# Denominator sums in pairs of heads on GpSimd, and VectorE multiplying the output bank out of PSUM

## What is computed

```python
def _tc_rmsnorm(x, t, gw, gb, bw, bb):
    g = (t @ gw.T + gb)[:, None, :]
    b = (t @ bw.T + bb)[:, None, :]
    inv_rms = jax.lax.rsqrt(jnp.mean(x * x, axis=-1, keepdims=True) + EPS)
    return g * x * inv_rms + b

def _attention(x, Wq, Wk, Wv, Wo):          # 16 heads of 32
    q, k, v = ...                           # x @ W.T, split into heads
    attn = jnp.einsum('blhd,bmhd->bhlm', q, k) / scale
    p = jax.nn.softmax(attn, axis=-1)
    o = jnp.einsum('bhlm,bmhd->blhd', p, v).reshape(B, L, D)
    return o @ Wo.T

x1 = x0 + _attention(_tc_rmsnorm(x0, t, ...), Wq, Wk, Wv, Wo)
y = x1 + silu(h @ gate_w.T) * (h @ hid_w.T) @ out_w.T    # h = _tc_rmsnorm(x1, ...)
out = x0 + y
```

## Time and profile before

| | us |
|---|---|
| median of 3 runs | 2371.1 |
| lowest, highest | 2369.59, 2376.34 |
| profiled execution | 2371.89 |
| its span | 2370.0 |

### The profile page before, as it was taken

How to read it: one execution, slowest core, us unless ns; L and a number is a source line. 1 busy time by engine, 2 the same in 40 slices (tenths; PEclk the granted TensorE clock), 3 DMA queues, 4 the chain that set the end, 5 groups by cost and what they waited for, 6 DMA issues and landing times.

```text
span 2370.0 us, 38915 instructions
## 1 busy us (share of the span) xinstructions
PE 2247.4 (95%) x10848; PEld 1565.9 (66%) x10848; DVE 1647.2 (70%) x2723; ACT 1283.8 (54%) x2286; POOL 1419.5 (60%) x1331
## 2 busy tenths in 40 slices
PE   5999989999989999899999889999999999999999
PEld 4655447555457554466554468887888788888887
DVE  4777745777736777546777378877887788778877
ACT  3367772567763667735666644363436344544454
POOL 0299981699952899915999846504660367036712
PEclk9999999999999999999999999999999999999999
DMA  6432213322132323132221331146114621363125
GB/s 192 149 96 64 83 34 99 88 77 65 59 103 51 97 56 90 32 112 66 64 54 32 111 138 54 39 153 210 54 36 134 222 65 36 111 201 109 43 88 179
DMA packets 96454, 221.94 MB, mean 94 GB/s; under 512 B 15712, under 2 KB 15712, under 8 KB 94560
## 3 DMA queue, kind: packets, MB, share of 16 engines
q1 hardware_dynamic: 95792, 212.93, 30.3%
q10 hardware_dynamic: 432, 6.29, 0.7%
HBM read 144.71 MB, written 24.12 MB: 71 GB/s over the span
## 4 chain that ended last, share of the span: by engine, by line
PE 75%; DVE 8%; issue 7%; ACT 4%; POOL 2%; SPq 2%; DMA 2%; DVEq 0%; ACTq 0%; POOLq 0%
PE bank L1869 26%; PE bank L1883 12%; PE bank L976 9%; PE bank L1100 8%; PE bank L1055 7%; PE bank L1161 6%; DVE pmax L800 3%; PE bank L1086 3%; PE bank L1065 2%; POOL sums L539 2%; SPq L381 2%; ACT qk_hi L617 1%; PE bank L1041 1%; DVE ow L1689 1%; DMA wo_raw<-in_out_w 1%
## 5 line engine op out<-in xcount | busy, mean ns | idle before, releaser
L800 DVE TENSOR_REDUCE pmax<-bank 128x1 f32<-128x512 f32 x1024 | 645.4, 683 | 177.5 <-PE bank L1055 171.5
L539 POOL TENSOR_TENSOR sums<-sums,probs_up 128x512 f32<-128x512 f32 x432 | 540.3, 1285 | 0.1
L1055 PE MATMUL bank<-ks,qs 96*128 96x512 f32 x1024 | 421.2, 422 | 36.2 <-DVE pmax L800 34.6
L1161 PE MATMUL bank<-qs,ks 128*128 128x512 f32 x1024 | 421.2, 416 | 15.0 <-ACT probs L701 8.3
L1883 PE MATMUL bank<-ow,aw 128*128 128x512 f32 x1536 | 360.6, 392 | 2.8 <-DVE ow L1689 2.7
L1869 PE MATMUL bank<-H_hi,wt_hi 128*128 128x512 f32 x896 | 350.5, 391 | 8.5 <-DVE H_lo L1724 8.3
L1869 PE MATMUL bank<-H_lo,wt_hi 128*128 128x512 f32 x896 | 349.8, 390 | 0.0
L1869 PE MATMUL bank<-H_hi,wt_lo 128*128 128x512 f32 x896 | 349.6, 390 | 0.0
L701 ACT ACTIVATE probs_up<-bank 128x512 f32<-128x512 f32 x512 | 283.3, 607 | 97.5 <-PE bank L1161 91.2
L701 ACT ACTIVATE probs<-bank 128x512 f32<-128x512 f32 x512 | 286.9, 602 | 86.3 <-PE bank L1161 78.7
L1883 PEld LDWEIGHTS bank<-ow,aw 128*128 128x128 f32 x1536 | 285.0, 188 | 65.3 <-issue 7.1
(11 more groups left out here) (184 smaller groups left out, 3559.3 us busy)
## 6 DMA issues: line engine op xcount, KB each, us to landing
raw<-in_gu_w SPq DMA_DIRECT2D x66, 512.0 KB, 3.8
wo_raw<-in_out_w SPq DMA_DIRECT2D x128, 256.0 KB, 2.8
qs<-qk_hi SPq DMA_DIRECT2D x256, 64.0 KB, 2.0
ks<-qk_hi SPq DMA_DIRECT2D x128, 128.0 KB, 2.4
x<-attn_out SPq DMA_DIRECT2D x10, 1024.0 KB, 9.2
x<-in_x SPq DMA_DIRECT2D x8, 1024.0 KB, 7.5
qs<-qk_lo SPq DMA_DIRECT2D x128, 64.0 KB, 2.0
ks<-qk_lo SPq DMA_DIRECT2D x64, 128.0 KB, 2.4
```

The costliest lines, as they stand in the source:

```text
L539: nc.gpsimd.tensor_tensor(total, first, probs(s, h), ALU.add) \
L800: nc.vector.reduce_max(pmax[:, t, h, hf:hf + 1], mbank[n % MB][:], AX_X).then_inc(sq_done, 1)
L1055: nc.tensor.matmul(mbank[n % MB][:], qs[0:96, u % 3, h, t * P:(t + 1) * P], ks[0:96, u // 2 % 2, h, hf * QB:(hf + 1) * QB], start=True, st ...
L1161: nc.tensor.matmul(sbank[i % SB][:], ks[:, g % 2, h, s * P:(s + 1) * P], qs[:, u % 3, h, :], start=True, stop=True).then_inc(st_ready, 1)
```

## The change

GpSimd's adds take two heads in one instruction (128 x 1024), 12 a unit. The place of the sums of heads 0 and 1 in quad 0 becomes the last quarter of `o` (group 3), except in unit 7, where all sums lie in `sums`, and the first add of each of its quads waits for the read of the one before. GpSimd's multiply goes. ScalarE's copies `output` and `denominators_up` go, and with them the semaphores `od_act`, `den_ready` and `den_up`. VectorE does all four parts of `normalise(u - 1)` in slots 6, 7, 8 and 9 of unit u, for u from 1 to 7, the second transpose now as a `link`; the last part multiplies `obank` by `den` and writes `o`. The values of pair 0 (slot 13) wait for that multiply. The last unit's normalisation stays where it was, in the new form.

```diff
+NORMALISE_AT = {(1, 2): 0, (1, 3): 1, (2, 0): 2, (2, 1): 3}
...
+HEADS = 2
+SUMS = QUADS * (QT - 1) * GH // HEADS
...
-    def sum_place(quad, h):
-        return yout[:, 0, :] if (quad, h) == (0, 0) else sums[:, h, :]
+    def probs_of(s, heads):
+        return probs_parts[s % 4 // 2][:, s % 2, HEADS * heads:HEADS * heads + HEADS, :]
+
+    def sum_places(u, quad, heads):
+        if u < NU - 1 and quad == 0 and heads == 0:
+            return o[:, NG - 1, :].rearrange("p (h c) -> p h c", h=HEADS)
+        return sums[:, HEADS * heads:HEADS * heads + HEADS, :]
...
-        def normalise(b, u):
-
-            pool.wait_ge(od_act, b * NU + (u + 2))
-            pool.wait_ge(den_ready, b * (NU - 1) + (u + 1))
-            cols = o[:, u // 2, u % 2 * QB:(u % 2 + 1) * QB]
-            nc.gpsimd.tensor_tensor(cols, cols, den[:], ALU.mult).then_inc(on_done, 1)
...
-                    if s == 4 and 0 < u < NU - 1:
-                        normalise(b, u - 1)
...
+                    for heads in range(GH // HEADS if s % QT else 0):
+
+                        pool.wait_ge(st_done, SCORES_T(b, NT + n * GH + HEADS * heads + HEADS) + SB)
...
+                        if s % QT == 1 and (heads == 1 or u == NU - 1):
 
                             pool.wait_ge(w_ready, MISC(b, sums_before(b, u, s // QT)))
...
+                        total = sum_places(u, s // QT, heads)
+                        first = probs_of(s - 1, heads) if s % QT == 1 else total
+                        nc.gpsimd.tensor_tensor(total, first, probs_of(s, heads), ALU.add) \
                             .then_inc(sum_done, 1)
...
-                        if (s, h) == (1, 1) and u:
-                            output(b, u - 1)
-                        if u == NU - 1 and (s, h) == (2, 3):
-                            denominators_up(b)
...
-            elif part == 2 and u == NU - 1:
+            elif part == 2:
                 link(nc.vector.transpose(den[:], pair[:, 1, :].unsqueeze(2).to_broadcast([P, QB // 32, 32])))
...
+                dve.wait_ge(pv_done, b * (NU * PAIRS) + (u + 1) * PAIRS + 2)
                 cols = o[:, u // 2, u % 2 * QB:(u % 2 + 1) * QB]
-                nc.vector.tensor_tensor(cols, cols, den[:] if u == NU - 1 else mspare[:], ALU.mult).then_inc(on_done, 1)
+                nc.vector.tensor_tensor(cols, obank[:], den[:], ALU.mult).then_inc(on_done, 1)
...
-                        if s == 3 and 0 < u < NU - 1 and h < 3:
-                            normalise(b, u - 1, h)
-                        if s == 2 and u == NU - 1 and h < 3:
-                            normalise(b, u - 1, h)
-                        if (u, s, h) == (NU - 1, 3, 0):
-                            normalise(b, u - 1, 3)
+                        if u and (s, h) in NORMALISE_AT:
+                            normalise(b, u - 1, NORMALISE_AT[s, h])
...
-                pe.wait_ge(od_act, b * NU + (u + 1))
+                pe.wait_ge(on_done, b * NU + (u + 1))
```

More of the change, by code:

```diff
@@ L165 @@
 SCORES_Q = Counter(0, NU * NMAX + NT)
-SUMS = QUADS * (QT - 1) * GH
+HEADS = 2
+SUMS = QUADS * (QT - 1) * GH // HEADS
 assert QT * QUADS == NS
-LINKS_PER_BATCH = NU * (2 + 2) + 1
+LINKS_PER_BATCH = NU * (2 + 3)
 HEAD_INC = 3 * 16
@@ L201, in sums_done @@
 def sums_done(b, u, s, h):
-    return b * (NU * SUMS) + (SUMS * (u + 1) + GH * (s // QT * (QT - 1) + max(s % QT, 1) - 1) + h + 1)
+    return b * (NU * SUMS) + (SUMS * (u + 1) + GH // HEADS * (s // QT * (QT - 1) + max(s % QT, 1) - 1) + h // HEADS + 1)
 def act_before(b, tile):
@@ L517, in batch @@
                         inverse_root(b, b * 2 + 3)
-                    if s == 4 and 0 < u < NU - 1:
-                        normalise(b, u - 1)
                     if n == NU * NS - 1:
                         pool.wait_ge(sum_done, sums_done(b, u, s - 1, GH - 1))
-                        pool.sem_inc(sum_done, GH)
+                        pool.sem_inc(sum_done, GH // HEADS)
                         break
[L525 to L531, removed]
+                    for heads in range(GH // HEADS if s % QT else 0):
+                        pool.wait_ge(st_done, SCORES_T(b, NT + n * GH + HEADS * heads + HEADS) + SB)
+                        if (u, s, heads) == (0, 1, 0):
+                            for w in range(2):
+                                pool.wait_ge(w_lo[w], 2)
+                        if s % QT == 1 and (heads == 1 or u == NU - 1):
                             pool.wait_ge(w_ready, MISC(b, sums_before(b, u, s // QT)))
                         if s % QT > 1:
[L536 to L539, removed]
+                            pool.wait_ge(sum_done, sums_done(b, u, s - 1, HEADS * heads))
+                        total = sum_places(u, s // QT, heads)
+                        first = probs_of(s - 1, heads) if s % QT == 1 else total
+                        nc.gpsimd.tensor_tensor(total, first, probs_of(s, heads), ALU.add) \
                             .then_inc(sum_done, 1)
@@ L548, in scalar_part @@
         act.sem_inc(st_done, ST_LEAD + SB)
-        act.sem_inc(od_act, 1)
         def square(b, hf, t):
@@ L696, in batch @@
                         act.wait_ge(st_ready, SCORES_T(b, i + 1))
-                        if s % QT != 1:
+                        if s % QT != 1 and h % HEADS == 0:
                             act.wait_ge(sum_done, sums_done(b, u, s - QT, h) if s >= QT
@@ L728, in batch @@
                             act.dma_start(wv[:].bitcast(F32), wv_dram).then_inc(wv_loaded, 16)
-            output(b, NU - 1)
             output_hi(b, len(SPLIT_AT))
@@ L1064, in denominators @@
             for h in range(GH):
-                last = nc.tensor.matmul(wbank[DH * h:DH * h + DH, :], ones[:], sum_place(quad, h), start=True,
+                last = nc.tensor.matmul(wbank[DH * h:DH * h + DH, :], ones[:], sum_places(u, quad, h // HEADS)[:, h % HEADS, :], start=True,
                                         stop=not direct)
@@ L1202, in attention_program @@
         "stacks": [(s, NB * NU * HEAD_INC) for s in q_stacked] + [(s, NB * NG * HEAD_INC) for s in k_stacked],
-        "values": [(pv_done, NB * NU * PAIRS + 2), (od_act, NB * NU + 1), (sum_done, sums_done(b, NU - 1, NS - 1, GH - 1))],
+        "values": [(pv_done, NB * NU * PAIRS + 2), (on_done, NB * NU + 1), (sum_done, sums_done(b, NU - 1, NS - 1, GH - 1))],
         "denominators": [(w_dve, MISC_DVE(b, dve_before(b, ("D", NU - 1, 1)) + 1))],
```

18 lines of the change are left out of this document (removed).

## The result

The changed kernel took 2414.6 us (median of four executions, 2407.7 to 2417.2), the kernel before beside it 2370.4: the ratio is 1.0171, 95% interval 1.0155 to 1.0187. The forecast was 2383.6 with a range from 2360 to 2397. The sign was right; the loss, forecast at 12.5 us, is 41 to 44.

What follows compares the result with a forecast made beforehand. TensorE, 95% busy, was taken as the bound, locally held by VectorE's reductions. Units 1 and 3 +19.2, unit 2 +6.8, unit 4 -5.6, unit 5 -0.35, unit 6 -7.1, unit 7 -0.4: +12.5 on 2371.1, 2383.6 us; range 2360 to 2397.

Steps and rivals of the forecast that it cites:

- The bound and the place: Units 1 and 3: VectorE's reduction of slot 10 gates slot 13's maxima product, then pair 0's values; +2.4 us each.
- rival 1: Slots 6 to 9, units 1 to 3: VectorE's added work absorbed, 0.6 us of 2.4 left; about 2358, chance 0.25.
- rival 2: GpSimd paces every unit through sums and denominators; 3 us per unit would go, 2330 us or below, chance 0.04.
- rival 3: A paired GpSimd add costs 2.8 us; waits for sums stay and about 5 us come on top, 2395, chance 0.08.
- the lower bound for the add: GpSimd's paired add costs at least 2.13 us: twice 1.285 less a whole 0.43 of fixed cost; 2.35 was taken.
- The burst: VectorE's four normalisation parts in slots 6 to 9: 2.4 us; +2.4 in units 1 and 3, +1.7 in unit 2.
- The second halves: Slots 14 to 21, freed of transposes and reciprocal: unit 4 -1.3 us in three batches, -1.7 in the last.
- The waits for sums: TensorE's 9.2 us of waits for GpSimd's sums all go: 7.0 in the last batch, the rest in unit 6.
- Units 5 and 6: Both halves over four batches, including sums' waits removed: unit 5 -0.35 us, unit 6 -7.1 us.

Runs made afterwards that it cites:

- the kernel with added products: Changed kernel plus 88 unread 512-column products in slots 10 to 13 of units 1 and 3 and 10 to 12 of unit 2: 2401.8 us.
- the shorter burst: Changed kernel without the first transpose and the reciprocal in units 1 to 7; second transpose and multiply stay in slots 8 and 9: 2381.6 us.

## Why the prediction was right or wrong

**The bound and the place: right.** "The chain through VectorE already sets this stretch": red(10) sets max(13), max(13) the values. Burst and waits lie where they were put, and rival 1 (absorbed), rival 2 (GpSimd paces every unit) and rival 3 (adds of 2.8 us) are all out: 2.6 us per burst arrive at TensorE in units 1 and 3, the pairs alone left these units at 0.0, and an add is 2.38. The 0.43 us of fixed cost in the lower bound for the add stands in no row; rows 3 give 1.285 - 512 x 0.00216 = 0.18. It did not enter the sum.

**The burst: right, a little small.** Units 1 and 3 at 2.4 became 2.6 (2.4 in the last batch): 20.6 for 19.2. Unit 2 at 1.7 became 2.0: 8.1 for 6.8. These are the numbers at the high clock.

**The second halves: right in size in unit 4, in part by luck.** Forecast was 0 for slots 6 to 13 and, for slots 14 to 21, -1.3 and in the last batch -1.7. Measured, from values to values, are +0.35 (+0.10 in the last batch) and -1.46, -1.88, -1.50 and -1.64; the whole first stretches sum to -5.3 for -5.6. But 1.1 of the 5.3 comes from an earlier transfer of keys, which the prediction did not have.

**The clock: the step that failed.** The prediction priced each wait by VectorE's queue alone and never asked what waits do to TensorE's granted clock. In the profiled execution that is 13.0 us (14.8 - 10.3 in unit 1, 18.8 - 10.3 in unit 3, by the kernel with added products), the largest term there is. The mean of 0.992 before could have raised the question. Most of what it lacks to 1.00 lies outside the attention units (0.93 over the 116 us ahead of them), but in unit 6's second stretch the clock is at 0.92 in the first batch and 0.91 in the third, 1.00 in the second, and the stretch lasts 17.83, 18.09 and 16.46 us. The Trainium skill, page "TensorE: Matmul & The Clock Gate", section "A second HAM failure mode: psum-queue depth-cycling", says that an engine that idles briefly and often between groups of products can swing between its two clock levels. The traces agree: here, four waits of 0.25 to 0.70 us in four slots.

Unit 2 has three of these waits, 0.59, 0.25 and 0.69, and no fourth, since a projection stands in slots 12 and 13; its clock stays at 1.00 in all four batches (2.06, 2.09, 2.13, 1.84):

```profile
512.00:516.00 4.00, 3.06 (x11) 1.84 (x12) 3.81 (x7) 1.49 (x4) 4.00 (x3) 1.00 0.77 169
516.00:520.00 4.00, 4.00 (x26) 1.92 (x25) 1.87 (x3) 0.91 (x2) 4.00 (x2) 1.00 0.07 14
```

That is no rule by the number of waits. Unit 5 of the last batch has three smaller ones (0.50, 0.16 and 0.60) and its stretch is at 0.90, and with the shorter burst two waits were enough in two of eight cases.

**The waits for sums: mis-sized.** Forecast: all 9.2 us go. Measured: 4.3 stay, 3.5 in units 5 and 6 and 0.8 in unit 7. The prediction had six adds of 2.35 run back to back once slot 21 is done. GpSimd in the last batch shows two of them standing apart:

```profile
1336.92 2.37 POOL L535 TENSOR_TENSOR sums<-probs 128x1024 f32<-128x1024 f32 x1
1340.99 2.36 POOL L535 TENSOR_TENSOR sums<-probs 128x1024 f32<-128x1024 f32 x1 [1.70 <-ACT probs L681]
1343.32 9.35 POOL L535 TENSOR_TENSOR sums<-sums,probs_up 128x1024 f32<-128x1024 f32 x4
```

The second pair waits for the exps of heads 2 and 3, which come after the values and denominators of slot 21; a sum of one head could start on head 2 alone. GpSimd idles 1.70 us there, ends at 1352.67, and the denominators wait 1.36 us for it. Making a piece of work coarser makes its start later: the 3 us of slack per unit were real, but lay behind this wait.

**Units 5 and 6: mis-sized.** Together forecast at -7.5, measured at about +2.9. Of the 10.4 between, 3.5 are the waits for sums that stayed. 2.5 are unit 6 in three batches: its slots 6 to 13 were put at 0 and cost 0.83 each (max(13) waits 0.46 for its reduction, at 315.47). 2.8 are unit 5's first stretches, 4.5 where the forecast has 1.6 (0.3 in each of three batches; in the last 2.4 - 0.7, less a wait for sums of 0.96 that did go); a fall of the clock in the last batch (0.90) is a part of it. The other 1.6 is in the main the clock again: unit 6's second stretch costs 1.9 us more over the first three batches, 1.65 of it in the second, where the granted clock was 1.00 before and is 0.91 after.

**The total.** 12.5 forecast, 13.0 of clock in units 1 and 3, 2.7 of burst in units 1 to 3, 0.7 in unit 4, 10.4 in units 5 and 6 and 0.5 in unit 7 make the 40 us of the ledger.

**What stays open.** Why the median execution is 7 us over the profiled one was not seen in a trace; its lower granted clock (0.980 to 0.983) points at more falls of the same kind. And why equal waits lower the clock in one batch and not in another (unit 1 in batch 1, unit 3 in the last, unit 4 above) was not settled; so the 13 us are the price of this execution, and another one can have more or fewer falls.

## What to carry to other kernels

When an edit puts waits into TensorE's stream, count them and price them twice: once as idle time, once as the products behind them at the lower clock. The second price came in six of eight cases here, so it belongs into the range as well as into the sum. Work moved to VectorE belongs in the units where TensorE has other work in those slots (here unit 4 alone, with the paired sums: -0.43%, of which -0.08% is the pairs'; the same edit in all units is +1.7%). And before making two steps into one, ask which of the two inputs comes last.

## What the runs showed of the hardware that was not expected

- Four waits of TensorE for VectorE, some 2.0 us in all and none over 0.70, were followed by a fall of the granted clock to its low level in six of eight cases; the values behind them took 3.12 us for 1.92 in the case shown. Three of the waits (1.5 us) were not, in four batches of unit 2, but two (0.69 and 0.46) were, in two batches with the shorter burst.
- Useless products in such waits made a kernel some 12 us faster, and cost 12.6 us where there were no waits.
- A 128x512 multiply on VectorE took 0.68 us with an operand in PSUM and 2.26 (median, up to 2.87) with both in SBUF. Each of the 29 that met a GpSimd add ended 0.55 us behind the add's end.
- ScalarE's copy of a projection had to wait 2.31 us for the transfer that reads the tile it writes; the unit's length followed the start of that copy within 0.02 us in nine cases of three kernels.
